# Scan of a vision layer on one core: the reciprocal product of the first state moved to GpSimd, the skip term moved to the experts, one block for the front

## The reference

```
h   = windowed_attention(x)                      # 8x8 windows, 8 heads of 8, rotary q and k, projection
u   = layernorm(h)
delta, B, C = split(u @ W_dbc, [16, 32]);  delta = softplus(delta @ W_dt + b_dt);  A = -exp(A_log)
for each of 16 states n:
    cum = exp(suffix sums of delta * A[:, n])
    y  += cumsum(delta * u * B[n] * cum, along the tokens) / (cum + 1e-12) * C[n]
h   = h + y + u * D                              # u * D is the skip term
out = h + relu(expert(argmax(router(layernorm(h)))))   # 32 experts, 64 -> 16 -> 64
```

## Time and profile before

| what | value |
|---|---|
| median of 3 runs | 610.61 us (608.54 to 611.0) |
| the profiled execution, its own time | 610.79 us |
| its span, first to last instruction | 609.0 us |
| busy share PE, DVE, ACT, POOL | 89%, 81%, 66%, 57% |
| mean granted clock of PE | 0.953 of 2.4 GHz |
| front block | 0 to 56.0 us of the span |
| attention | 56.2 to about 281 us |
| scan, with its preparation | 281 to 397 us; the eight and one blocks of the two states from 338.6 us |
| experts | 397.1 to 609.0 us |

### The profile page before, as it was taken

The page is one execution under the profiler, slowest core; times in us unless marked ns, Lnnn a source line. Parts: engine busy times, 40 slices in busy tenths (PEclk is TensorE's granted clock), DMA queues, the critical chain, the costliest instruction groups (busy, mean ns, idle before and its releaser), DMA issues. The chain is left out here.

```text
span 609.0 us, 18377 instructions
## 1 busy us (share of the span) xinstructions
PE 541.0 (89%) x7273; PEld 391.1 (64%) x7274; DVE 493.6 (81%) x911; ACT 403.9 (66%) x723; POOL 349.8 (57%) x388
## 2 busy tenths in 40 slices
PE   5797999999999999999557676759999999999996
PEld 4797889999988899998212232435555555555553
DVE  4887688888888888885798999858888888888873
ACT  3575788888888888889596676325454545454543
POOL 8303367777779877774799499653333333333320
PEclk9898799999999999999797889869999999999999
DMA  9732222222222222210000000000010101111111
GB/s 193 111 43 46 55 59 64 56 61 59 57 61 58 56 62 59 55 44 10 1 0 0 0 1 1 3 2 18 18 28 20 26 21 25 22 23 23 24 23 27
DMA packets 62382, 23.06 MB, mean 38 GB/s; under 512 B 45780, under 2 KB 62292, under 8 KB 62292
## 3 DMA queue, kind: packets, MB, share of 16 engines
q1 hardware_dynamic: 61200, 21.63, 17.5%
q10 hardware_dynamic: 964, 0.20, 0.2%
q0 software_dynamic: 128, 0.00, 0.0%
HBM read 5.02 MB, written 4.19 MB: 15 GB/s over the span
## 5 line engine op out<-in xcount | busy, mean ns | idle before, releaser
L762 DVE TENSOR_REDUCE work<-psum 128x16 f32<-128x1024 f32 x64 | 78.0, 1220 | 31.6 <-PE psum L597 31.6
L697 ACT ACTIVATE work<-work 128x1024 f32<-128x1024 f32 x64 | 67.8, 1060 | 23.1 <-DVE work L767 23.1
L767 DVE TENSOR_TENSOR work<-psum,work 128x1024 f32<-128x1024 f32 x64 | 78.4, 1225 | 2.2
L705 ACT ACTIVATE work<-psum 128x512 f32<-128x512 f32 x128 | 70.9, 619 | 3.1 <-PE psum L612 2.2
L612 PE MATMUL psum<-kc,work 128*128 128x128 f32 x512 | 68.6, 278 | 3.2 <-ACT work L697 2.8
L1681 POOL TENSOR_TENSOR m_rstd<-m_var,m_mhalf 128x4 f32<-128x4 f32 x32 | 32.2, 1008 | 61.9 <-DVE m_var L1889 61.9
L628 PEld LDWEIGHTS psum<-work 128*64 128x64 f32 x2048 | 62.3, 138 | 5.4 <-issue 5.1
L628 PE MATMUL psum<-work 128*64 128x18 f32 x2048 | 65.5, 212 | 0.0
L612 PEld LDWEIGHTS psum<-kc,work 128*128 128x128 f32 x512 | 59.8, 143 | 7.5 <-ACT work L697 2.9
L1704 PE MATMUL psum<-x_t,w1x 64*64 64x256 f32 x1024 | 64.4, 390 | 0.0
L484 POOL TENSOR_TENSOR work<-work,kc 128x512 f32<-128x512 f32 x32 | 41.9, 1309 | 38.5 <-DMA work<-big_bc 26.8
(11 more groups left out here) (198 smaller groups left out, 1281.2 us busy)
## 6 DMA issues: line engine op xcount, KB each, us to landing
work<-big_bc SPq DMA_DIRECT2D x256, 32.0 KB, 2.0
h_all<-in_x SPq DMA_DIRECT2D x16, 256.0 KB, 5.3
work<-big_a SPq DMA_DIRECT2D x32, 128.0 KB, 2.2
out<-out_st SPq DMA_DIRECT2D x126, 32.0 KB
w1x<-in_L_ffn_W SPq DMA_DIRECT2D x2, 128.0 KB, 4.2
kc<-constants SPq DMA_DIRECT2D x1, 202.0 KB, 2.8
w2x<-in_L_ffn_W SPq DMA_DIRECT2D x1, 128.0 KB, 3.5
work<-in_L_tok_qkv_w ACTq DMA_DIRECT2D x2, 32.0 KB, 3.5
```

Of the source, the lines that this page charges most:

```text
L697: act.activation(prob[:, f], prob[:, f], ACT.Exp).then_inc(prob_done, 1)
L705: act.activation(prob_t[:, f, 4 * half:4 * half + 4, :].rearrange("p j q -> p (j q)"), banks[4 + half][:, :], ACT.Copy).then_inc(prob_t_do ...
L762: dve.tensor_reduce(top[:, f, :].rearrange("p (g h) -> p g h", g=4), sc, AX.X, ALU.max).then_inc(top_done, 1)
L767: dve.tensor_tensor(prob[:, f].rearrange("p (g h) k -> p g h k", g=4), sc, top[:, f, :].rearrange("p (g h) -> p g h", g=4).unsqueeze(3).br ...
```

## The change

It has four parts.

1. **Scan, first state.** DVE's `ratio` pass goes to POOL as `times_rec`, which multiplies the sum by the reciprocal straight into `y`. DVE's `out` pass becomes `times_c`, in place on `y`, and is issued one block late: behind the term and the sums of the next block. POOL's `add` goes for these eight blocks, since nothing is in `y` before. The reciprocal goes to one of two SBUF buffers instead of PSUM, and the logarithm from block 1 on to PSUM. The second state keeps the old passes.
2. **Skip term.** ACT's L1175 goes from the scan. In the experts ACT makes D * u + bias for one quad into `skip_st`, and POOL adds `y` to it into `y_st` (`stage_y`); before, ACT copied. POOL does the first of these before `ident_b` and `off`.
3. **Experts.** PE turns `y` ahead of the masks and into another PSUM bank, behind ACT's copy of the marks.
4. **Front.** Front and attention become one block. `w_delta` and `a_neg` are made in steps 20 to 24 of the q and k loop. The rotary bias takes four small DVE instructions instead of six. POOL's constants for scan and experts, made before in quads 18 and 20 of the attention, are made ahead of it.

```diff
             def recip(q):
                 act.wait_ge(lnc_done, q + 1)
-                if isinstance(q, int) and q == 0:
-                    act.wait_ge(tail_gain, 4)
+            if isinstance(q, int) and q < 2:
+                act.wait_ge(tail_bc, 8)
+            elif isinstance(q, int) and q <= BLOCKS:
+                act.wait_ge(ratio_done, q - 1)
                 else:
                     act.wait_ge(ratio_done, q)
-                act.activation(psum[:, 5:7, 0:BLK], log_cum, ACT.Exp, scale=-1.0).then_inc(rec_done, 1)
+            act.activation(rec_of(q), log_of(q), ACT.Exp, scale=-1.0).then_inc(rec_done, 1)
...
+        def times_rec(blk):
+
+            pool.wait_ge(sum_done, blk + 1)
+            pool.wait_ge(rec_done, blk + 1)
+            pool.tensor_tensor(block_of(y, blk), cums[blk % RING], rec_of(blk), ALU.mult).then_inc(ratio_done, 1)
...
             with pool.If(alive_of[0][0] > 0):
                 duc(0, 0, 0)
+            duc(1, 1, 1)
+            tail_product(0)
                 for k in range(BLOCKS - 1):
-                    duc(k + 1, k + 1, (k + 1) % RING)
-                    add(k, k)
-                    if 1 <= k < 5:
+                times_rec(k)
+                if k < BLOCKS - 2:
+                    duc(k + 2, k + 2, (k + 2) % RING)
+                if 2 <= k < 5:
                         tail_product(k - 1)
...
+        def times_c(blk):
+
+            dve.wait_ge(ratio_done, blk + 1)
+            dve.wait_ge(c_done, blk + 1)
+            dve.tensor_tensor(block_of(y, blk), block_of(y, blk), psum[:, 2:4, 0:BLK], ALU.mult).then_inc(out_done, 1)
...
             with dve.If(alive_of[0][0] > 0):
-                whole(0)
-                carry(0, (BLOCKS - 1) % RING)
+            add_up(0, 0, True)
+            for k in range(1, BLOCKS):
+                add_up(k, k % RING, False)
+                times_c(k - 1)
+            carry(0, (BLOCKS - 1) % RING, BLOCKS)
...
                 with dve.If(alive_of[1][1] > 0):
-                    body(BLOCKS, BLOCKS % RING, True)
-                    carry(1, BLOCKS % RING)
+                add_up(BLOCKS, BLOCKS % RING, True)
+                carry(1, BLOCKS % RING, BLOCKS + 1)
+                kept_back()
+                finish(BLOCKS, BLOCKS % RING)
...
+            def stage_y(i):
+
+                pool.wait_ge(skip_made, i + 1)
+                if not first(i):
+                    pool.wait_ge(y_turned, i)
+                pool.tensor_tensor(y_st[:, :, :].rearrange("p k (r x) -> p k r x", r=8),
+                                   skip_st[:, :, :].rearrange("p k (r x) -> p k r x", r=8),
+                                   raster(y, i // 2 * 512 + i % 2 * 32), ALU.add).then_inc(y_staged, 1)
+
+            stage_y(0)
...
+                if live(i, -1):
+                    pe.wait_ge(y_staged, i + 2)
+                    if not first(i, -1):
+                        pe.wait_ge(h_done, i + 1)
+                    if live(i, 2):
+                        pe.wait_ge(mark_act, i - 1)
+                    for n in range(2):
+                        m = pe.transpose(psum[:, 2, 256 + n * P:256 + n * P + P], y_st[:, n, :], ident)
+                    m.then_inc(y_turned, 1)
```

More of the change, by code:

```diff
@@ L656, in values @@
             pe.wait_ge(x_staged, i * 16 + 16)
-            if not first(i):
+            if first(i):
+                pe.wait_ge(t["qk_act"], 32)
+                pe.wait_ge(t["qk_dve"], 32)
+            else:
                 pe.wait_ge(prob_t_done, i * 4)
@@ L823, in carve, with both_stages @@
     return take
-def both_stages(nc, ctx, t, work, moe):
-    router_w, router_b, w1, b1, w2, b2 = moe
+def both_stages(nc, block, ctx, t, work):
     w1x, w2x, b1c, b2p, b2r, rwx, rb_row, rw = (
@@ L1339, in _ @@
                 kept_back()
-                for k in range(BLOCKS - 1):
-                    duc(BLOCKS + k + 1, k + 1, (BLOCKS + k + 1) % RING)
-                    add(BLOCKS + k, k)
-                add(2 * BLOCKS - 1, BLOCKS - 1)
+                add(BLOCKS, BLOCKS - 1)
+                pool.wait_ge(duc_done, BLOCKS + 1)
+                skip(pool, mine, BLOCKS + 1, BLOCKS - 1)
             with pool.Else():
-                with pool.If(alive_of[1][1] > 0):
-                    duc(BLOCKS, BLOCKS - 1, BLOCKS % RING)
-                    kept_back()
-                    add(BLOCKS, BLOCKS - 1)
-                    pool.wait_ge(duc_done, BLOCKS + 1)
-                    skip(pool, mine, BLOCKS + 1, BLOCKS - 1)
@@ new lines, in _, with start @@
+                kept_back()
+                pool.wait_ge(out_done, BLOCKS)
+                skip(pool, mine, BLOCKS, BLOCKS)
+        def start(n):
+            for s in (c_done, rec_done, out_done, y_added):
+                pool.wait_ge(s, n * BLOCKS)
+            pool.wait_ge(tail_y, n * 2 + 1)
+            pool.tensor_copy(a_n[:, :], a_neg[:, bass.ds(n, 1)]).then_inc(rep_staged, 1)
+            pool.wait_ge(rep_staged, n * 5 + 1)
+            for w, at in ((w_b[0], RANK), (w_c[0], RANK + NS)):
+                for b in range(2):
+                    q = slice(64 * b, 64 * b + 64)
+                    pool.tensor_copy(w[q, q], wd[q, bass.ds(n + at, 1)].to_broadcast([64, 64])
+                                     ).then_inc(rep_staged, 1)
+            pool.wait_ge(rep_staged, n * 5 + 5)
@@ L1733, in body @@
                         pe.wait_ge(o_copied, i - 2)
-                    pe.wait_ge(h_done, min(i + 1, QUADS))
+                    if not first(i, 3):
+                        pe.wait_ge(out_made, i - 3)
                     for n in range(2):
```

1124 lines of the change are left out of this document (570 added, 554 removed).

## The result

| | before | after |
|---|---|---|
| median | 610.04 us (608.54 to 611.0) | 652.65 us (650.33 to 656.93) |
| profiled execution, own time and span | 610.79, 609.0 us | 650.33, 648.6 us |

The ratio of after to before is 1.0708, 95% interval 1.0671 to 1.0744: 43 us slower. I had forecast 639 us (624 to 648). The direction was right and the size was not. Where the time went is read from the trace in three stretches.

What follows compares the result with a forecast made beforehand. The prediction took DVE to bound the scan (busy 54.9 of 58.5 us). Scan 33.2 us lost, less 4.1 for the front and 0.5 for the experts, is 28.6 lost on 610.79: 639 us, range 624 to 648.

Steps and rivals of the forecast that it cites:

- The wait in the scan: Scan: DVE waits seven times, before the terms of blocks 2 to 8, for PE's C then B; 33.2 us lost.
- The clock step: Scan, PE: after 5.0 us idle each group of eight starts at 1.2 GHz, so C and B take 5.35 us, not 3.65.
- The 3.4 us that the sum used for every group: Scan, PE: the low-clock stretch at the start of each group, in which 1.7 us of work get done.
- The rival at full clock: Scan: the wait is there but PE keeps its full clock, period 8.70 us, 626 us in all; chance 0.12.
- the one at low clock throughout: Scan: rival with the low clock for each whole group, period 12.05 us, 654 us in all; chance 0.06.
- PE's sum of the tail as the new last link: End of the scan: PE's sum, hidden before, now comes behind C of block 8 and ends at 428.3 us.
- The front: Ahead of the scan: bias, removed stop, first scores and POOL's moved constants together gain 4.1 us (2.5 to 5.8).
- the bias: Front, DVE: four small bias instructions instead of six gain 0.6 us (bounds 0 and 1.0).
- The experts: Experts: 1.7 us lost at the start against 2.2 us gained by the turn of `y`, together 0.5 us gained.
- POOL's addition in each step is hidden in its idle time (57% busy): Experts, each step: POOL's added pass costs nothing, as POOL is 57% busy.
- 1.7 us lost once: Start of the experts: POOL's two additions, 0.63 us each, and about 0.4 us waiting for ACT's skip term.
- the turn ahead of the masks: Experts, PE: turning `y` earlier fills PE's wait for the marks, 0.08 us in 28 steps, 2.2 us gained (0 to 5).

## Why the prediction missed

The profile's own sum closes: scan +32.6, what stands ahead of it -9.0, experts +16.0 make the 39.6 us between the two spans. With the front at the 3.8 us of its own run it is 44.8 us, against 43 us of the ratio.

- **The wait in the scan** held in every part, and its sum closes. Place: ahead of the terms of blocks 2 to 8, seven times. Cause: C between `times_c` and B, shown by the run with B first. C and B together 5.35 us forecast and 5.35 measured; period 10.40 forecast and 10.24 measured; loss 33.2 forecast and 32.6 measured.
- **The clock step** held in size: 1.7 us a group forecast, and measured in five of seven (5.35 against 3.65 us); and the run with PE kept at work gives 8.50 us for the 8.70 forecast at full clock. The 3.4 us that the sum used for every group are shown as a fixed length by no run; what the runs show is the loss, 1.7 us in five groups and 2.1 and 2.0 in the two others. Nor did each group start at the low clock: two of seven did, the others fell to it within their first half us. The forecast's choice had less under it than it seems. It set "the rows with 2.0 to 2.4 us idle" beside a period of 8.70, but those rows are the ones with the low clock; and it did not show the C group of block 6, which ran at full clock behind 2.47 us of idle:

```profile
375.09 1.96 PE L1020 MATMUL psum<-u_all,w_c 128*128 128x504 f32 x4 [2.47 <-DVE work L1506]
```

  So that the clock would fall behind 5.0 us was a fair bet and not a reading. The rival at full clock (626 us) falls by these rows, and so does the one at low clock throughout (654 us), though the total came near that number: it did so for a reason in another stage. By its own terms, moreover, that rival comes to 440.5 at the end of the scan; its 444 needs PE's sum of the tail at the low clock too, 3.84 us more, which it doesn't say.
- **PE's sum of the tail as the new last link** held: it starts at 414.95 and DVE waits 3.13 us for it.
- **The front**, 4.1 us forecast (2.5 to 5.8), holds by the run with the front alone, 3.8 us (2.3 to 5.3). Of its terms the bias was undersized: 0.6 us, at most 1.0, for what the traces show as 2.4 us on DVE and 1.7 to 3.6 us at the first copy of q or k, though what it is worth in the total is not settled. So the sum for the front came out right with a term that was too small in it, and in part by luck. How the rest divides was not tried.
- **The experts are the step that failed**: 0.5 us gained was forecast, 16.0 lost measured. Two terms did it. The first is the sentence "POOL's addition in each step is hidden in its idle time (57% busy)". It was hidden on POOL, yes; but I asked only whether POOL had room, and not what DVE does in the same moment. The addition holds up two DVE passes by 0.63 us, DVE becomes the bound, and the step grows by 0.42 us: 10.3 us over the steps behind the second. The second is one that the sum put at nothing. "1.7 us lost once" for the start was right, 1.9 us from the last of the scan to the first mark (12.5 to 14.4), but the first two steps lost 3.8 more (7.13 + 8.56 against 5.71 + 6.16). They are short without the addition (5.86 and 6.18), long with it even where it overlaps no DVE pass (6.47 and 8.47), and short again with it once PE is kept at work (5.98 and 6.15), so the low clock of the first full step is shown as what makes them long. Why the clock is low there is not settled. PE's idle time ahead of the first marks is 0.45 to 0.49 us without the addition and 0.88 to 1.30 with it, but with the one-input copy it is 1.19 us and the clock is full (second layer 1.90 us). Nor did the turn ahead of the masks give its 2.2 us: in the table of steps it costs 0.05 to 0.20 us each.
- **The range** ended at 648, and its only bounds for the experts' steps were 0 and 5 us of gain, for the turn. No loss was allowed for an engine that gets a new pass beside another engine's. That is what made it miss.

The Trainium skill has the rule that I should have weighed. "SBUF — State Buffer", section "Who interferes with whom", says that a DVE instruction with two inputs in SBUF contends with a GpSimd instruction that reads SBUF, and that the port pair the two share is an exclusive lock. The trace agrees: 0.72 and 0.58 us instead of 0.29, each ending behind POOL's pass, and the copy with one input did it as well.

## What to carry to other kernels

Before a pass is moved to an idle engine, lay its new place over the other engines' timelines: idle share says whether it fits there, not whom it holds up; for POOL look at DVE's passes with two inputs in SBUF in that window, and move it to a window with one-input or PSUM passes. Before a pass is reordered, write down for each in-order queue what stands between the releasing instruction and the product that is wanted next; here the same products in another order were worth 38 us. And where a stage's first steps run at TensorE's low clock, products that nobody reads can shorten them, if they are sized from the trace to fit into the idle time.

## What the runs showed of the hardware

- DVE's passes with two inputs in SBUF ended 0.13 to 0.15 us behind POOL's pass when they came upon it: behind an addition of 0.73 us, a square of 0.66 and a copy of 0.40. A pass of 0.29 us lost up to 0.43.
- The length of the idle time before a group did not decide its clock. Six products behind the same 1.71 us of idle took 2.84 us in one run and 4.54 in another; the prediction had read idle of 1.38 us as harmless and 2.00 us as harmful from one row each. In the trace of before, C behind 2.40 to 2.47 us of idle took 3.49, 2.58, 1.96 and 3.65 us. Behind 4.85 to 5.33 us of idle all eight C groups of the scan after the change took 3.2 to 3.7 us instead of 1.96.
- The same front placed the start of the scan at 329.45 to 333.91 us, so one profile can mislead by 4 us about a stage, while the medians of five rounds settle it to 1.5.
